# Context stage of a perceiver block: four places in place of two for the broadcast deviations, their write and spread one pair sooner, and its steps laid out

## The reference

```python
# 1: context part: cosine of every token with every context row (256 of them)
v = layernorm(x) @ Wv.T + bv            # 256 -> 128
t = ctx @ Wt.T + bt                     # 192 -> 128
x = x + (v @ t.T) / max(|v| |t|, 1e-8)  # 64 x 256 per sequence
# 2: attention, 16 heads of 16, within a sequence; the part of o along v is removed
o = softmax(q @ k.T / 4) @ val
o = o - (sum(o * val) / (sum(val * val) + 1e-8)) * val
x = x + o @ wo.T + bo
# 3: 14 experts, each token by the argmax of its router logits, gelu, weight softmax(logits)[argmax]
x = x + weight * (gelu(x @ w1[e] + b1[e]) @ w2[e] + b2[e])
```

## Time and profile before

| | us |
|---|---|
| median of 3 runs | 500.67 |
| lowest, highest | 498.14, 501.09 |
| the profiled execution | 500.66 |
| its span | 498.8 |
| around the span | 1.86 |

### The profile page before, as it was taken

How to read it: one execution, slowest core, us unless ns; L and a number is a source line. 1 busy time by engine, 2 the same in 40 slices (tenths; PEclk the granted TensorE clock), 3 DMA queues, 4 the chain that set the end, 5 groups by cost and what they waited for, 6 DMA issues and landing times.

```text
span 498.8 us, 14061 instructions
## 1 busy us (share of the span) xinstructions
PE 483.6 (97%) x4316; PEld 387.8 (78%) x4317; DVE 337.0 (68%) x1024; ACT 332.5 (67%) x809; POOL 245.2 (49%) x430
## 2 busy tenths in 40 slices
PE   8999999998999999999999999989999999999995
PEld 6544444566888888888888888768989999999994
DVE  4577675657889989998998999988573333333331
ACT  3765565569998898889889988977354334334331
POOL 2468754344344465566646555552674333332332
PEclk9999999999999999999999999999999999999999
DMA  8989998500001222322231122156475766666620
GB/s 308 266 210 291 252 300 246 174 2 2 1 2 39 84 57 92 97 96 63 87 97 62 53 66 58 52 148 207 160 225 190 243 217 198 223 215 190 217 89 30
DMA packets 35361, 69.98 MB, mean 140 GB/s; under 512 B 6672, under 2 KB 22034, under 8 KB 35296
## 3 DMA queue, kind: packets, MB, share of 16 engines
q1 hardware_dynamic: 31456, 60.06, 40.9%
q0 software_dynamic: 3408, 8.85, 4.7%
q10 hardware_dynamic: 432, 0.26, 0.3%
HBM read 58.27 MB, written 11.48 MB: 140 GB/s over the span
## 4 chain that ended last, share of the span: by engine, by line
PE 64%; DVE 6%; issue 4%; ACT 3%; POOL 2%; POOLq 0%; ACTq 0%; DVEq 0%
PE psum L1532 12%; PE psum L1545 11%; PE psum L1459 9%; PE psum L1436 6%; PE psum L1423 6%; PE psum L1415 6%; PE psum L1383 5%; PE psum L1488 5%; PE psum L1282 5%; DVE arena L912 1%; POOL out L614 1%; POOL tok L528 1%; ACT arena L1145 0%; DVE smax L901 0%; ACT arena L1181 0%
## 5 line engine op out<-in xcount | busy, mean ns | idle before, releaser
L1532 PEld LDWEIGHTS psum<-arena,ring 128*128 128x128 f32 x624 | 75.5, 192 | 2.6 <-issue 0.6
L1532 PE MATMUL psum<-arena,ring 128*128 128x128 f32 x624 | 76.1, 275 | 0.5 <-issue 0.5
L1545 PE MATMUL psum<-w_s,arena 128*128 x312 | 73.8, 380 | 0.0
L1215 ACT ACTIVATE arena<-psum 128x256 f32<-128x256 f32 x39 | 15.0, 385 | 84.0 <-PE psum L1282 79.4
L1036 DVE SCALAR_TENSOR_TENSOR arena<-psum,slot_rec,arena 128x256 f32<-128x256 f32 x39 | 18.9, 484 | 71.7 <-PE psum L1545 71.4
L556 POOL TENSOR_TENSOR ov<-o_n,v_s 128x256 f32<-128x256 f32 x32 | 26.1, 817 | 77.8 <-DVE o_n L794 77.8
L1545 PEld LDWEIGHTS psum<-w_s,arena 128*128 128x128 f32 x312 | 56.4, 190 | 6.3
L1181 ACT ACTIVATE arena<-kT,head_mask 128x256 f32<-128x256 f32 x128 | 59.3, 531 | 0.0
L614 POOL DMA_INDIRECT out<-arena,token_of x39 | 39.8, 1022 | 19.3 <-POOL token_of L606 14.6
L901 DVE TENSOR_REDUCE smax<-psum 128x16 f32<-128x1024 f32 x32 | 39.2, 1224 | 12.6 <-PE psum L1436 12.6
L1221 ACT ACTIVATE arena<-psum,b_s 128x128 f32<-128x128 f32 x156 | 44.4, 375 | 3.5 <-PE psum L1532 2.2
(11 more groups left out here) (206 smaller groups left out, 1074.7 us busy)
## 6 DMA issues: line engine op xcount, KB each, us to landing
ring<-w SPq DMA_DIRECT2D x39, 512.0 KB
w_s<-ctxT SPq DMA_DIRECT2D x15, 768.0 KB, 10.0
w_s<-w SPq DMA_DIRECT2D x16, 448.0 KB, 3.6
slot_rec<-routed SPq DMA_DIRECT2D x39, 132.0 KB, 3.7
tok<-x SPq DMA_DIRECT2D x16, 256.0 KB, 9.0
w_s<-xT SPq DMA_DIRECT2D x12, 256.0 KB, 7.4
routed<-pad_rec SPq DMA_DIRECT2D x1, 1980.0 KB, 8.7
tok<-b SPq DMA_DIRECT2D x14, 128.0 KB, 3.1
```

The costliest lines, as they stand in the source:

```text
L1532: mm = pe.matmul(hid_bank(p)[:, f * P:(f + 1) * P], w1_s[:, r, c * F + f * P:c * F + (f + 1) * P], xgT[:, p, c * P:(c + 1) * P], start=c = ...
L1545: mm = pe.matmul(bank(2 + q, D), hidT[:, q, f * P:(f + 1) * P], w2_s[:, bass.ds(e * (FC * D) + f * D, D)], start=f == 0, stop=f == FC - 1)
```

## The change

`std_b` gets four places (SPREAD = 4) and `wvc_s` moves further on in the arena; there are four `std_in` and four `std_out` semaphores, and places are n % 4. The spread of pair n waits for `v_sbuf` of n - 3 in place of n - 1.

SyncE's step i from 7 on issues, after x transposed and the context of pair i: the spread of pair i - 1, the write of pair i + 1, x of pair i + 3. In steps 5 and 6 x comes first, then the spread of i - 1, then the write of i + 1; in step 4 the writes of pairs 4 and 5 come at its end. After the last step only the spread of pair 15 is left. The loops of GpSimd, DVE, ScalarE and TensorE in this stage (one round of four steps; two rounds on ScalarE) are laid out one by one.

```diff
--- before.py
+++ after.py
@@ -43,6 +43,7 @@
 ZEROED, CONSTS = 4, 12
 TURNED = 4
 AHEAD = 6
+SPREAD = 4
 LO, HI = 8, 28
 RING, RLO, RHI = 8, 12, 28
 RESTS = 12
@@ -192,8 +193,8 @@
 
         arena = sb("arena", [P, 10560])
         vT, vsq = (arena[:, 4096 + n * 2 * D:4096 + (n + 1) * 2 * D].rearrange("p (s j) -> p s j", s=2) for n in range(2))
-        std_b = arena[:, 2048:2048 + 4 * P].rearrange("p (s j) -> p s j", s=2)
-        wvc_s = arena[:, 2048 + 4 * P:2048 + 4 * P + KC * H].rearrange("p (c h) -> p c h", c=KC)
+        std_b = arena[:, 2048:2048 + 8 * P].rearrange("p (s j) -> p s j", s=SPREAD)
+        wvc_s = arena[:, 3328:3328 + KC * H].rearrange("p (c h) -> p c h", c=KC)
         pair_rstd, pair_rvar, pair_std = (arena[:, 3072 + n * NT:3072 + (n + 1) * NT] for n in range(3))
         norm, rnorm, cos = (arena[:, 5120 + n * 4 * SC:5120 + (n + 1) * 4 * SC].rearrange("p (s j) -> p s j", s=2)
                             for n in range(3))
@@ -296,8 +297,8 @@
 
         x_in = [sem(f"x_in{n}") for n in range(4)]
         ctx_in = [sem(f"ctx_in{n}") for n in range(4)]
-        std_in = [sem(f"std_in{n}") for n in range(2)]
-        std_out = [sem(f"std_out{n}") for n in range(2)]
+        std_in = [sem(f"std_in{n}") for n in range(SPREAD)]
+        std_out = [sem(f"std_out{n}") for n in range(SPREAD)]
         rec_out = [sem(f"rec_out{n}") for n in range(RING)]
         rec_in = [sem(f"rec_in{n}") for n in range(RECS)]
         w1_in = [sem(f"w1_in{n}") for n in range(4)]
@@ -344,30 +345,37 @@
                         sp.dma_start(xT_s[:, k], xT[bass.ds(i, 1)].rearrange("o p j -> (o p) j")).then_inc(ctx_in[k], 16)
                     sp.dma_start(ctx_in_sb[:, k], ctxT[bass.ds(i, 1)].rearrange("o p j -> (o p) j"))\
                         .then_inc(ctx_in[k], 16)
-                def turned(n):
-                    return isinstance(n, int) and not TURNED <= n < NB
-                if not turned(i - 2):
-                    spread_deviations(i - 2, k % 2)
+                if i >= TURNED + 3:
+                    spread_deviations(i - 1)
+                    if i + 1 < NB:
+                        write_deviations(i + 1)
                 for n in (i + 2,) if i < 4 else (i + 2, i + 3) if i == 4 else (i + 3,):
                     if n < NB:
                         load_x(n, n % 4)
-                if not turned(i):
-                    need(sp, s["a_std"], i - TURNED + 1)
-                    sp.dma_start(deviations[bass.ds(i, 1)].rearrange("o p h -> (o p) h"), pair_std[:, bass.ds(i * 2, 2)])\
-                        .then_inc(std_out[k % 2], 16)
+                if TURNED < i < TURNED + 3:
+                    spread_deviations(i - 1)
+                if i == TURNED:
+                    write_deviations(TURNED)
+                if TURNED <= i < TURNED + 3:
+                    write_deviations(i + 1)
                 if 8 <= i < 8 + RESTS // 2:
                     for to, source in rest[2 * (i - 8):2 * (i - 7)]:
                         sp.dma_start(to, source).then_inc(s["consts_in"], 16)
 
-            def spread_deviations(n, q):
-                need(sp, std_out[q], arrivals(n - TURNED, q, 2, 16))
-                need(sp, s["v_sbuf"], n - 1)
+            def write_deviations(n):
+                sp.wait_ge(s["a_std"], n - TURNED + 1)
+                sp.dma_start(deviations[bass.ds(n, 1)].rearrange("o p h -> (o p) h"), pair_std[:, bass.ds(n * 2, 2)])\
+                    .then_inc(std_out[n % SPREAD], 16)
+
+            def spread_deviations(n):
+                q = n % SPREAD
+                sp.wait_ge(std_out[q], arrivals(n - TURNED, q, SPREAD, 16))
+                need(sp, s["v_sbuf"], n - SPREAD + 1)
                 sp.dma_start(std_b[:, q, :], deviations[bass.ds(n, 1)].rearrange("o p h -> o (p h)").broadcast_to([P, 2 * P]))\
                     .then_inc(std_in[q], 16)
             for i in range(NB):
                 load_tokens(i, i % 4)
-            for n in (NB - 2, NB - 1):
-                spread_deviations(n, n % 2)
+            spread_deviations(NB - 1)
 
 
             sp.wait_ge(s["consts_made"], CONSTS)
@@ -584,7 +592,7 @@
                     v_i = v_s[:, k % 4, :].rearrange("p (h d) -> p h d", h=NH)
                     pool.tensor_tensor(vv[:, :, 0:HD], v_i, v_i, ALU.mult).then_inc(s["vv_ok"], 1)
                 return send
-            run_steps(pool, context_step, -4, NB - 1, 6, 10)
+            lay_steps(context_step, -4, NB - 1)
             pool.wait_ge(s["consts_in"], 16 * RESTS)
             pool.wait_ge(s["consts_made"], CONSTS)
             attention_step(0, 0)
@@ -690,11 +698,12 @@
                 if paired(v) and not (isinstance(v, int) and v < TURNED):
                     need(dve, s["v_psum"], v + 1)
                     need(dve, s["dots_psum"], v - 1)
-                    need(dve, std_in[p], arrivals(v - TURNED, p, 2, 16))
+                    r = (k + 1) % SPREAD
+                    need(dve, std_in[r], arrivals(v - TURNED, r, SPREAD, 16))
                     if isinstance(v, int) and v == TURNED:
                         dve.wait_ge(s["first_made"], 6)
                     dve.scalar_tensor_tensor(vT[:, p, :].rearrange("f (h t) -> f h t", h=2),
-                                             std_b[:, p, :].rearrange("f (t h) -> f h t", h=2), xbs_s[:, :],
+                                             std_b[:, r, :].rearrange("f (t h) -> f h t", h=2), xbs_s[:, :],
                                              bank(p, 2 * P).rearrange("f (h t) -> f h t", h=2), ALU.mult, ALU.add)\
                         .then_inc(s["v_sbuf"], 1)
 
@@ -912,7 +921,7 @@
                     dve.tensor_tensor(prob[:, (k - 1) % 2, :].rearrange("p (h j) -> p h j", h=NH), s_ps,
                                       smax[:, :].unsqueeze(2).broadcast_to([P, NH, S]), ALU.subtract)\
                         .then_inc(s["centred"], 1)
-            run_steps(dve, context_step, -4, NB - 3, 6, 10)
+            lay_steps(context_step, -4, NB - 3)
             attention_step(-1, 3)
             context_step(NB - 3, NB - 3)
             context_step(NB - 2, NB - 2)
@@ -1200,7 +1209,7 @@
                     exponentiate(u, (k - 1) % 2)
                 if live(u):
                     spread_second_values((k - 1) % 2, (k - 1) % 4)
-            run_steps(act, context_step, -1, NB, 4, 12)
+            lay_steps(context_step, -1, NB)
             context_step(NB, NB)
             act.wait_ge(s["consts_in"], 16 * RESTS)
             act.wait_ge(s["vd_ones"], 9)
@@ -1509,7 +1518,7 @@
                 if live(y):
                     need(pe, s["xT_ok"], i + 2, NT)
                     turn_output(y, (k - 3) % 2)
-            run_steps(pe, context_step, -1, NB, 8, 12)
+            lay_steps(context_step, -1, NB)
             pe.wait_ge(s["consts_made"], CONSTS)
             attention_step(0, 0)
             context_step(NB, NB)
```

## The result

The changed kernel takes 503.5 us in the median of 8 runs (501.21 to 505.97), the kernel before 499.97 us (497.84 to 508.45, 8 runs). The ratio is 1.0077, with a 95% interval of 1.0053 to 1.0100: slower by 3.9 us, or 2.7 to 5.0. The profiled execution took 504.38 us, with a span of 502.6; before it was 500.66 and 498.8, so the two executions differ by 3.7 us and their spans by 3.8. The difference is under 1%, and its interval is clear of 1. The run of 508.45 us was a slow one, and the ratio leaves it out.

A forecast was written before the change was run, and what follows sets the result against it. The prediction took TensorE to bound the context stage. Its terms, -0.7 for the stall won, +2.2 for x of pair 9, +1.0 for pair 10 and 0 for the rest, gave +2.5 on 500.66, so 503.2 us, range 499.0 to 506.1.

The forecast's parts named there:

- What bounds the stage, and what could be won: Context stage, about 8 to 104 us: TensorE bounds it, busy 95.31 of 96 us, so only 0.69 us can be won.
- The term of -0.7: TensorE's stall before the norm matmuls goes as spreads land sooner: -0.7 us, bounds 0 and -0.7.
- x of pair 9: Load queued behind pair 6's write lands at 40.6, 3.2 us late for DVE; TensorE loses 2.2 us, bounds 0 and 2.2.
- x of pair 10: Load waiting behind a_std of pair 8, issued at 37.3, lands between 44.6 and 48.5; loss 1.0 us, bounds 0 and 1.95.
- x of pairs 11 to 15: Later loads, each behind a_std of a pair two lower, come in time: 0 us taken, bounds 0 and 1.3.
- just holds: DMA's load of one later step: 3.7 us of bytes and at most 2.0 for a write, 5.7 of 5.94 us.
- Laid-out steps: Laying out the engines' loops in the context stage: 0 us taken, bounds -0.3 and +0.3.
- The sum: All terms together: +2.5 us on the profiled execution's 500.66 us, which is 503.2.
- The rule weighed: Skill's price for small descriptors, on the transfer itself: 8-byte elements cost nothing that counts; the forecast followed the profile's rows instead.

The follow-up runs named there:

- the four places alone: Kernel before with four places and the spread's wait for v_sbuf of n - 3, nothing else: 499.34 us, ratio 0.9998 to the kernel before.
- the run with loops: Changed kernel with the old loops of its four engines put back: 503.07 us, ratio 1.0083 to the kernel before.
- x first from step 7 on: Changed kernel with x ahead of the spread and the write from step 7 on, pair 6's write unmoved: 502.0 us, ratio 1.0069 to the kernel before.
- the first experiment: Changed kernel with only the write of pair 6 moved behind the loads of step 6: 501.2 us, ratio 1.0049 to the kernel before.
- with x first: Changed kernel, x ahead of spread and write from step 7 on: alone 502.0 us; with pair 6's write behind step 6's loads 498.68, again 499.51.
- one write: Changed kernel with the deviations' write left out for all pairs but pair 4, whose write every spread reads: 499.26 us, one run.
- wide ones: Changed kernel, all spreads reading pair 4's write, the eleven others replaced by unread writes of 128 x 512 bytes: 499.78 us, one run.
- the run with unread small writes: Changed kernel, all spreads reading pair 4's write, the eleven others sent as 128 x 8 bytes to an unread tensor: 505.9 us, one run.

## Why the prediction was right, point by point

The number was right, and so were the mechanism and the place of each stall; the sizes of the terms were not, and their errors cancelled in part.

- **What bounds the stage, and what could be won.** Right: TensorE, and about its idle time. The term of -0.7 came out as -0.83 in the trace, and the four places alone bring -0.81.
- **x of pair 9.** Right in each link, and somewhat too large: issue foreseen at 32.65 (32.70), landing at 40.6 (40.2), late for DVE by 3.2 (2.65, counted from DVE's own readiness at 37.6), hidden by 0.95 of that (1.0), TensorE idle by 2.2 (1.64).
- **x of pair 10.** Landing foreseen at 44.6 to 48.5; it was issued at 37.26 and landed 9.1 later, at 46.4. The term was 1.0 us of TensorE's time, and in the profiled execution it was 0, since DVE, held up by the slow matmuls, reads this x only at 46.84. Where the clock did not fall the wait is there, and costs TensorE less than half of the term: 1.18 us of DVE's and 0.44 of TensorE's in the run with loops, 1.03 and 0.28 with x first from step 7 on.
- **x of pairs 11 to 15.** This term was mis-sized: 0 was taken out of bounds of 0 and 1.3, and 1.65 was measured, at pair 15, outside the bounds. The forecast had seen that the weights of steps 11 and 12 overfill the queue, and took the step that "just holds" (5.7 of 5.94 us) as the nearer row. That step was too tight a sum. It spread the 23.5 us lost over 12 writes, but of the 12 only 10 are issued between 20 and 86 us, and an eleventh at 19.82; over these it is 2.1 to 2.35 us a write, and the step comes to 5.8 to 6.05. In the first experiment pairs 12 and 14 are late too, by 1.59 and 1.29 us. That pair 15's x is late by the order and the writes together is shown by its wait with x first (0.77 and 0.85 us, none of it at TensorE), and by there being none with one write or wide ones.
- **The clock.** Not foreseen: no term had it, and it cost 1.8 us in this execution.
- **Laid-out steps.** 0, as far as the run with loops can tell.
- **The sum.** +2.5 was forecast; +4.27 was measured at step 15 of the trace, +3.7 over the whole execution, +3.5 between the medians, +3.9 by the ratio. At step 15 the forecast had 0.6 too much for pair 9 and 1.0 for pair 10, and lacked 1.65 for pair 15 and 1.8 for the clock. That 503.2 stands beside a median of 503.5 is luck besides: the forecast started from 500.66, the profiled execution of the kernel before, whose median in the runs beside the changed kernel is 499.97.
- **What a run without a fall of the clock costs.** Three of the changed kernel's eight runs have a mean clock of 0.999 or 1.000, which leaves no room for a fall like that at 42 us (0.43 of full missing over 4 us are 1.7 in 502.6, 0.0034 of the mean). They took 501.21, 502.86 and 502.91 us, against a lowest of 497.84 before, so the loss is not the clock's alone. How the medians' 3.5 us divide among the stalls is open, since the changed kernel has one trace.
- **The rule weighed.** The Trainium skill (DMA: Bandwidth & Descriptors, Why small descriptors are slow (HBM only)) prices a small descriptor by itself. The traces do not agree with the reading that this is all: with 8-byte writes the DMA moved 132 GB/s from 32 to 38 us, with 512-byte ones 245, and what was dear was the time of the loads behind.

## What to carry to other kernels

In a queue that issues in order, count what stands behind each wait, not what the wait is for: a result sent one step sooner took 8 us of lead (an issue at 32.70 in place of 24.66) from loads that had nothing to do with it. Put the load with the nearest deadline ahead of the wait, and a tiny scattered write last. And before shortening a wait, ask how much of it reaches the engine that bounds the stage: here it was 0.7 of 7.0 us. And compare traces at the end of the stage that was changed: here two later pieces, untouched by the change, moved the span by 1.5 us one way and 1.9 the other.

## What the runs showed of the hardware

- Behind the write of 128 x 8 bytes at 31.3 us, which took 3.7 and 3.8 us to land, the loads of the same queue all but stopped: they moved 13 and 11 GB/s from 32 to 35 us, against 253 behind a write of 128 x 512 bytes, which landed after 1.5 us. x of pair 9 landed in 7.5 and 8.0 us with the small writes, 4.7 without, 5.1 with the wide ones. Why the small ones do so is open.
- After a pause of 1.64 us at 40.5 us TensorE's clock fell, for the most part to its lower level (a mean of 0.57 from 42 to 46 us, matmuls of 1.06 us taking 1.9 to 2.0). After pauses of 1.58 and, in the run with unread small writes, of 2.09 us its matmuls kept 1.09. Between 333 and 339 us all eleven traces have the same pause of 1.5 to 1.6 us, and in six of them the clock falls behind it (0.91 from 330 to 350 us) and in five it does not (1.00), at a price of some 1.5 us. So the length of the pause does not decide it, and a stall's price is its idle time plus, at times, as much again.
- From GpSimd's last instruction to the end of the span it took 2.6 us in seven traces and 4.5 to 4.65 in four, whatever the version.
